# One step table of a two-layer attention kernel: the negated maxima of the first half in step 19 instead of 20

## The reference, cut to what matters

```python
x = x + tanh(g_xattn[0]) * attention(layernorm(x), ctx, w_qkv, w_proj, b_proj)   # 16 heads of 16, softmax over 120 + 256 keys
x = x + tanh(g_ffn[0])   * ternary_linear(layernorm(x), weight, bias)            # input rounded to int8 by max |x| over all batches
x = x + tanh(g_xattn[1]) * depool(layernorm(x), ctx, ...)                         # a linear layer and a recurrence over 120 patches
x = x + tanh(g_ffn[1])   * int8_linear(layernorm(x), rhs)
```

```python
s = (q * scale) @ k.T          # 256 x 376, in fp32
p = exp(s - max(s, axis=-1))   # the row maximum is exact in this kernel
out = (p @ v) / p.sum(-1)
```

## Time and profile before

| | us |
|---|---|
| median of 3 runs (lowest to highest) | 1109.1 (1106.7 to 1109.81) |
| the profiled execution | 1110.44 |
| its span, first to last instruction | 1108.6 |
| PE busy in the span | 1033.3 (93%) |
| DVE busy | 875.8 (79%) |
| ACT busy | 798.8 (72%) |
| POOL busy | 697.1 (63%) |

### The profile page before, as it was taken

One profiled execution on the slowest core, in us unless ns is written; L12 is line 12 of the kernel. 1 busy time (PEld: TensorE's weight loads), 2 busy tenths in 40 slices (PEclk: granted clock), 3 DMA queues, 4 the chain that ended last, 5 costly groups with the idle time before them and its releaser, 6 DMA issues. The chain is left out here.

```text
span 1108.6 us, 26277 instructions
## 1 busy us (share of the span) xinstructions
PE 1033.3 (93%) x8522; PEld 709.7 (64%) x8522; DVE 875.8 (79%) x2218; ACT 798.8 (72%) x1731; POOL 697.1 (63%) x1348
## 2 busy tenths in 40 slices
PE   4889999999999999999999999999999977999994
PEld 3456666666666666666666666666666545788873
DVE  6657778877877778877877888778877765899996
ACT  3367777777777777777777777777777746999983
POOL 6556666666666666666666666666666214677776
PEclk8689999999999999999999999999999996999997
DMA  7654444444444444444444444444443210223332
GB/s 149 94 111 106 113 107 108 107 107 104 105 104 105 104 107 116 107 105 104 109 105 107 109 111 116 106 107 109 98 97 91 77 32 20 73 93 110 95 107 81
DMA packets 159339, 111.30 MB, mean 100 GB/s; under 512 B 17698, under 2 KB 155364, under 8 KB 159204
## 3 DMA queue, kind: packets, MB, share of 16 engines
q1 hardware_dynamic: 158212, 108.89, 41.0%
q10 hardware_dynamic: 992, 0.74, 0.4%
HBM read 30.33 MB, written 16.32 MB: 42 GB/s over the span
## 5 line engine op out<-in xcount | busy, mean ns | idle before, releaser
L926 DVE TENSOR_REDUCE neg<-ms_ps 128x1 f32<-128x376 f32 x1024 | 527.2, 544 | 176.2 <-PE ms_ps L686 170.1
L1016 ACT ACTIVATE probs<-st_ps 128x512 f32<-128x512 f32 x768 | 443.2, 600 | 29.6 <-PE st_ps L676 26.2
L686 PE MATMUL ms_ps<-k,q 96*128 96x376 bf16 x1024 | 335.6, 329 | 10.5 <-DMA q<-parts 5.8
L676 PE MATMUL st_ps<-q,k 99*128 99x256 bf16 x1536 | 295.3, 274 | 14.2 <-DMA q<-negT 14.1
L676 PEld LDWEIGHTS st_ps<-q,k 99*128 99x128 bf16 x1536 | 132.8, 98 | 143.3 <-issue 41.9
L701 PE MATMUL pv_ps<-probs,v 128*32 128x256 f32 (+1 forms) x3072 | 194.5, 383 | 0.0
L724 PE MATMUL misc<-xnT,wqkvT 128*128 128x256 f32 x512 | 156.1, 388 | 1.8 <-DVE wqkvT L808 1.1
L686 PEld LDWEIGHTS ms_ps<-k,q 96*128 96x128 bf16 x1024 | 99.1, 97 | 70.4 <-DVE neg L926 43.4
L701 PEld LDWEIGHTS pv_ps<-probs,v 128*32 128x32 f32 (+1 forms) x3072 | 96.1, 110 | 55.9 <-issue 13.9
L546 POOL TENSOR_SCALAR parts<-qk 128x632 bf16<-128x632 f32 x63 | 45.2, 718 | 126.2 <-ACT qk L1084 126.2
L724 PEld LDWEIGHTS misc<-xnT,wqkvT 128*128 128x128 f32 x512 | 92.9, 196 | 6.8 <-ACT qk L1064 1.8
(11 more groups left out here) (201 smaller groups left out, 1754.9 us busy)
## 6 DMA issues: line engine op xcount, KB each, us to landing
k<-parts SPq DMA_DIRECT2D x379, 94.0 KB, 3.2
q<-parts SPq DMA_DIRECT2D x384, 64.0 KB, 3.0
out_dram<-xn SPq DMA_DIRECT2D x32, 256.0 KB, 2.2
xs<-in_x SPq DMA_DIRECT2D x31, 256.0 KB, 2.9
cx<-in_ctx SPq DMA_DIRECT2D x32, 240.0 KB, 3.8
recurrence_input<-u_in SPq DMA_DIRECT2D x32, 120.0 KB, 2.8
plug<-plugs SPq DMA_DIRECT2D x32, 120.0 KB, 3.4
powers<-gath SPq DMA_DIRECT2D x32, 120.0 KB, 2.0
```

The source lines that it names most:

```text
L676: mm = pe.matmul(st_ps[u % SR][:, j * S:(j + 1) * S], k6[0:KM, r, h, k * P:(k + 1) * P], q6[0:KM, r, h, :], start=True, stop=True)
L686: pe.matmul(ms_ps[t][:, 0:KEYS], q6[0:KR, r, h % HU, t * P:(t + 1) * P], k6[0:KR, r, h % HU, 0:KEYS], start=True, stop=True).then_inc(s_ms, 1)
L926: dve.tensor_reduce(neg[:, m, t, h % HU:h % HU + 1], ms_ps[t][:, 0:KEYS], AX.X, ALU.max, negate=True).then_inc(s_red, 1)
L1016: act.activation(probs[:, u % PR, :], st_ps[u % SR][:, :], ACT.Exp).then_inc(s_exp, 1)
```

## The change

Only tables of numbers change. PE's table (`JOBS`) and the number of score tiles per step:

```diff
-            "o1": (1, 16, 1, 0), "neg0": (1, 20, 1, 1), "o2": (1, 22, 1, 0),
+            "o1": (1, 16, 1, 0), "neg0": (1, 19, 1, 1), "o2": (1, 22, 1, 0),
...
-            counts = [1, 1, 1, 2, 2, 1] * NG
+            counts = [1, 2, 1, 2, 1, 1] * NG
```

More of the change, by code:

```diff
@@ L327, in flamingo_two_layers @@
         JOBS = {
[3 rows of a table removed]
[3 rows of a table added]
         }
         AT = {
-            "cxp": 0, "xnT": 1, "copy_o": 2, "kc": 4, "csq": 5, "q": 6, "aT": 5, "neg1": 7, "xn": 13, "k": 11, "decay": 17,
-            "vcx": 14, "neg0": 19, "v": 23,
-            "stats0": 0, "aggr0": 5, "norm": 4, "update": 19, "stats1": 20, "aggr1": 23, "mx": 6, "mn": 7,
+            "cxp": 2, "xnT": 1, "copy_o": 4, "kc": 4, "csq": 5, "q": 8, "aT": 5, "neg1": 6, "xn": 9, "k": 11, "decay": 21,
+            "vcx": 13, "neg0": 18, "v": 23,
+            "stats0": 1, "aggr0": 5, "norm": 4, "update": 18, "stats1": 19, "aggr1": 20, "mx": 7, "mn": 5,
         }
```

## The result

| | before | after |
|---|---|---|
| median of 4 runs (lowest to highest) | 1107.98 us (1106.7 to 1109.81) | 1131.16 us (1127.37 to 1133.2) |
| profiled execution | 1110.44 us | 1127.37 us |
| its span | 1108.6 us | 1125.6 us |

The kernel before has one run more here than in the table ahead. The ratio after to before is 1.0204 (95% interval 1.0171 to 1.0237). A second comparison of the same two kernels gave 1.0179 (1.0159 to 1.0199). So the change makes the kernel about 2% slower, 20 to 23 us. I had forecast 8 us slower (1117), with 1123 as the upper end of the range: the direction was right, the size was not.

A forecast was written before the change was run, and what follows sets the result against it. PE was taken to bound the kernel: a bare batch of 26.91 us plus 0.20 of wait gives 27.11 against 26.85, +0.26 over 30 batches, +8 us, so a median of 1117 us (own range 1113 to 1121; 8 in 10: 1105 to 1123).

The forecast's parts named there:

- my chain of rows: Steps 11 to 13: later o0 delays DVE's reciprocal and first maximum, so PE's step 13 tile starts 0.52 us later per batch.
- neg0's wait for POOL: Step 19: PE asks for neg0 before POOL has its parts, a wait of 0.18 us a batch (0.05 to 0.3).
- neg0 ahead of a group: neg0 moved from step 20 to ahead of step 19's attended group saves 0.22 us of PE's issue a batch.
- q: ACT's copy of q, now behind neg1's, comes late for k's first part on PE: loss 0.19 us (0.05 to 0.24).
- kcT: ACT's copy of cxp, now behind two exponentials and xnT, delays PE's kcT: loss 0.08 us (0 to 0.17).
- The wait left at step 0: PE's remaining wait for neg0's rows at the batch's start: 0.20 us on the mean of 28 batches.
- the sum for a bare batch: Batch without a wait at step 0: 26.21 + 0.08 + 0.07 + 0.19 + 0.52 - 0.12 + 0.18 - 0.22 = 26.91 us.
- aT: aT comes behind a DVE with one tile more to reduce ahead of o3: loss 0.07 us (0 to 0.1).
- cost nothing: Other moves (copies of o0 to o2, xn, proj, decay, DVE's statistics) were to fall into slack or idle time: no cost.
- the faster one: Rival: ACT and DVE run ahead of the chain, small waits do not come; batch 26.70 us, 1104 to 1105; chance 0.16.
- Slower still, by neg0's wait: Rival: at step 19 POOL's parts are late by the full 0.3 us, all bounds met; +16 us, 1125; chance 0.07.
- Much faster: Rival: arrival hangs on neg0, so step 0's wait goes and neg0 is cheaper; -26 us, 1083; chance 0.02.

The follow-up runs named there:

- q alone late: Kernel before with only ACT's copies of q and neg1 moved, to steps 8 and 6; ratio to before 1.0203, batch 27.47 us.
- o0 and POOL mended: Changed kernel with o0 divided on DVE in step 11 and POOL's first-half split_neg ahead of the bias; ratio to before 1.0029, batch 26.82 us.
- o0 mended: Changed kernel with DVE's division of o0 one step later, in step 11; ratio to before 1.0151, batch 27.22 us.
- POOL mended: Changed kernel with POOL's split_neg of the first half ahead of the bias of x; ratio to before 1.0155, batch 27.09 us.
- both with SP: Changed kernel with o0 divided in step 11, POOL's split_neg first, SP issuing neg0's rows ahead of the first stack's last two DMAs; ratio to before 0.9902.
- POOL and SP changed on the kernel before: Kernel before with POOL's split_neg ahead of the bias and SP issuing neg0's rows ahead of the first stack's last two DMAs; ratio 0.9889, batch 26.33 us.

## Why the prediction was wrong

**Right.** PE's wait at step 0 hangs on SP's queue and k's copy, not on neg0's copy (but for 7 of 28 batches). DVE stands before o0, and PE's step 13 tile waits 0.64 us behind it, 0.58 more than before, where my chain of rows had 0.52. neg0's wait for POOL: 0.17 for 0.18. neg0 ahead of a group, where it has no wait: 0.23 saved for 0.22. q: 0.22 for 0.19. kcT: 0.07 for 0.08. The wait left at step 0: 0.13 for 0.20.

**The step that failed** is the sum for a bare batch, 26.91 us, and in it the terms ahead of the copy of k. The mechanism stands; terms of it were put at nothing or taken too small. On the mean of the 28 batches the batch less its wait at step 0 went from 26.23 to 27.15 us, +0.92, where the sum has +0.70. (27.22 less 26.21 would give 1.0, but batch 21 had a wait at its start, as said above. The prediction took its 26.21 for any batch and called the batches alike in every other place; those with no wait at their start were 0.12 longer.) The prediction put the copy of k 0.12 us later in the batch; it is 0.31 later on the mean. Left out were xT behind the copy of v (0.07 us) and the tile of step 4 behind DVE (0.08). aT was taken at 0.07 and is 0.11, q at 0.19 and is 0.22. Behind the copy of k, step 13 was taken at 0.52 and is 0.58. And neg0's move, -0.22 + 0.18 in the sum, saved nothing: step 20 is 0.31 us shorter and step 19 0.30 longer, since the wait for POOL lengthens that step by more (0.23) than the 0.17 between the two matmuls. Together these are 0.3 us; hundredths in many other places take 0.1 of it back.

Most of a delay ahead of the copy of k counts, as the run with q alone late showed. The terms for xT and for the tile of step 4 are read from the traces; no run took either away. The first of them was hidden before: the wait at step 0 gave ACT time to finish the copy of v. Where that wait is back, in the run with o0 and POOL mended, xT and kcT wait for nothing. So part of the 0.5 us that the change gained at step 0 was paid back at step 1. The miss in the batch is 0.18 us, as the wait left at step 0 is 0.07 smaller than forecast: 27.29 for 27.11, 5 us in 28 batches.

**The second error** is in the number of places. I counted 30 batches at 0.26 us and nothing elsewhere. The start, the first two and the last batch run through the same tables and cost 3 to 7 us together. In the profiled pair it is 4.6 us. With nearly 5 us of the batches, and 5 us by which the medians lie further apart than forecast and result of the profiled execution (1118.5 and 1127.37), it makes the 14 us between 1117 and 1131. Those last 5 us are scatter, and the runs do not say why it fell so.

**What the sum hid.** I listed step 13 with 0.52 and neg0 with 0.18 as if to mend the first would bring 0.52. The runs show the bounds to be parallel: o0 mended brings 0.07 us a batch, POOL mended 0.20, both 0.47, both with SP 0.93. The remark that proj, the copies of the groups and DVE's statistics "cost nothing" held in the changed kernel. But the copies are harmless only together with the early neg0, and neg0's move pays only together with DVE's earlier steps.

Rivals: the faster one (the small waits do not come) is out, since they came and more. "Slower still, by neg0's wait" had nearly the right size (1125) but not the right place: neg0's wait was as forecast, 0.17 us. "Much faster" (1083) is out with it. The new counts of tiles per step and the earlier xn were never moved by themselves.

The Trainium skill's page "DMA: Bandwidth & Descriptors", section on queues, rings and completion order, has the completion of a DMA behind the earlier writes of its DMA engine. Issuing neg0's rows ahead of two stack DMAs made the wait go, which agrees with it. It does not prove it, since the issue itself came earlier too. The run with POOL and SP changed on the kernel before holds that time nearly fixed: rows issued at 23.78 to 23.79 us of the batch behind ten of the stack's DMAs kept PE waiting in none of 28 batches. In the 7 batches of before in which SP waited for the copy they were issued at 23.66 to 23.79 behind all twelve, and PE waited 0.3 to 0.7 us in 3 of them. But the DMA ahead of the rows had been issued 0.9 to 2.7 us earlier in that run and 0.7 to 1.4 us earlier in these 7, so this agrees with the rule too and does not prove it. No row shows the landing of these rows.

## What to carry to other kernels

Where an in-order engine waits at the end of a loop for something that starts in the middle of the loop, most of a delay ahead of that start counts (here 0.63 of 0.78 us), and the wait at the end is hardly any slack for it. Find the operation from which the parallel ways part (here the copy of k) and compute each way to where they meet again; to mend one of them brings only the difference to the next. A small job that moves to another step takes its neighbours on two other engines with it: check for each, in the new order, who stands in front of it and what that one waits for.

## What the runs showed of the hardware that was not expected

A transposing matmul pair of 24 columns costs PE about 0.30 us of issue between a step's float32 job and the next scores, and 0.07 to 0.08, where it has no wait, ahead of the attended group of float32 matmuls on 32 columns (step 20 against step 19, in three kernels). SP's issues stand 0.64 us apart, but in most batches one of the thirteen takes 0.4 to 1.4 us more, at changing places. This moved the issue of neg0's rows between 23.7 and 25.2 us of the batch, and from the issue to step 0 it took 2.2 to 3.2 us; the two together made the wait at step 0 vary from 0 to 1.8 us before. The runs do not show why either of them varies.
